# One chain of 128 features in place of two interleaved halves of 64, in the step of an LSTM

## The reference

```python
# x [32, 512, 512], cond_1024 [32, 512] is h0, Wx and Wh [512, 2048], b [2048]
xW = jnp.einsum('ntd,dg->ntg', x, Wx) + b
c0 = jnp.zeros_like(h0)
def step(carry, xw_t):
    prev_h, prev_c = carry
    a = xw_t + prev_h @ Wh
    i = jax.nn.sigmoid(a[:, :Hd])
    f = jax.nn.sigmoid(a[:, Hd:2 * Hd])
    o = jax.nn.sigmoid(a[:, 2 * Hd:3 * Hd])
    g = jnp.tanh(a[:, 3 * Hd:])
    next_c = f * prev_c + i * g
    next_h = o * jnp.tanh(next_c)
    return ((next_h, next_c), next_h)
(_, _), hs = jax.lax.scan(step, (h0, c0), jnp.swapaxes(xW, 0, 1))
return x + jnp.swapaxes(hs, 0, 1)
```

## Time and profile before

| | |
|---|---|
| time, median of 3 runs | 2726.16 us (2726.15 to 2726.85) |
| the profiled execution's own time | 2726.29 us |
| its span, first to last instruction | 2724.5 us |
| mean granted TensorE clock | 0.989 of full speed |
| TensorE matmuls, busy | 2671.2 us (98%), 49152 |
| VectorE, busy | 1929.8 us (71%), 8121 instructions |
| ScalarE, busy | 1245.7 us (46%), 3722 instructions |
| GpSimd, busy | 45.9 us (2%) |
| chain of work that ended last | TensorE 97% |
| HBM traffic | 40 GB/s over the span |

### The profile page before, as it was taken

The page is one execution under the profiler, slowest core; times in us unless marked ns, Lnnn a source line. Parts: engine busy times, 40 slices in busy tenths (PEclk is TensorE's granted clock), DMA queues, the critical chain, the costliest instruction groups (busy, mean ns, idle before and its releaser), DMA issues.

```text
span 2724.5 us, 121148 instructions
## 1 busy us (share of the span) xinstructions
PE 2671.2 (98%) x49152; PEld 1387.0 (51%) x49152; DVE 1929.8 (71%) x8121; ACT 1245.7 (46%) x3722; POOL 45.9 (2%) x134
## 2 busy tenths in 40 slices
PE   3999999999999999999999999999999999999998
PEld 0455555555555555555555555555555555555554
DVE  6777777777777777777777777777777777777776
ACT  3444444444444444444444444444444444444444
POOL 0000000000000000000000000000000000000000
PEclk6999999999999999999999999999999999999999
DMA  6111111111111111111111111111111111111111
GB/s 144 37 43 35 38 38 40 35 39 42 35 38 38 40 35 39 42 35 38 38 39 35 39 42 35 39 38 39 35 39 42 35 39 39 38 35 39 42 36 26
DMA packets 223520, 109.94 MB, mean 40 GB/s; under 512 B 25216, under 2 KB 222464, under 8 KB 222464
## 3 DMA queue, kind: packets, MB, share of 16 engines
q1 hardware_dynamic: 223488, 109.48, 15.7%
HBM read 75.83 MB, written 33.55 MB: 40 GB/s over the span
## 4 chain that ended last, share of the span: by engine, by line
PE 97%; issue 1%; DVE 1%; DMA 1%; SPq 0%; ACT 0%; POOL 0%; DVEq 0%; POOLq 0%
PE Z L244 97%; DMA wx_raw<-in_Wx 1%; DVE wh_lo L435 0%; SPq L213 0%; SPq L200 0%; DVE wmax L417 0%; SPq L208 0%; DVE h_hi L475 0%; ACT tanh_c L356 0%; POOL wmax_all L537 0%; DVE xmax L396 0%; DVE x_lo L381 0%; DVE zs L407 0%; DVE c L490 0%; DVE scales L410 0%
## 5 line engine op out<-in xcount | busy, mean ns | idle before, releaser
L350 ACT ACTIVATE act<-Z,scales 128x192 f32<-128x192 f32 x1022 | 430.9, 422 | 1159.5 <-PE Z L244 1159.5
L244 PE MATMUL Z<-wx_hi,x_hi 128*32 128x512 f16 x8176 | 807.7, 379 | 9.3 <-DVE x_lo L381 9.3
L244 PE MATMUL Z<-wh_hi,hT_hi 128*32 128x512 f16 x8176 | 808.1, 379 | 8.0 <-DVE hT_hi L480 8.0
L244 PE MATMUL Z<-wh_lo,hT_hi 128*32 128x512 f16 x8176 | 808.1, 379 | 0.0
L244 PE MATMUL Z<-wx_hi,x_lo 128*32 128x512 f16 x8176 | 807.6, 379 | 0.0
L244 PE MATMUL Z<-wx_lo,x_hi 128*32 128x512 f16 x8176 | 807.6, 379 | 0.0
L244 PE MATMUL Z<-wh_hi,hT_lo 128*32 128x512 f16 x8176 | 533.1, 379 | 0.0
L486 DVE TENSOR_TENSOR fc<-act,c 128x64 f32<-128x64 f32 x512 | 115.3, 225 | 570.2 <-ACT act L350 570.2
L356 ACT ACTIVATE tanh_c<-c 128x64 f32<-128x64 f32 x1024 | 262.3, 256 | 269.7 <-DVE c L497 249.2
L475 DVE SCALAR_TENSOR_TENSOR h_hi<-act,scales,tanh_c 128x64 f16<-128x64 f32 x1024 | 291.3, 285 | 113.1 <-ACT tanh_c L356 86.3
L327 ACT ACTIVATE Z<-bias_bc,scales 128x512 f32<-128x512 f32 x511 | 344.6, 674 | 0.0
(11 more groups left out here) (50 smaller groups left out, 1286.1 us busy)
## 6 DMA issues: line engine op xcount, KB each, us to landing
x_in<-in_x SPq DMA_DIRECT2D x512, 64.0 KB, 2.0
x_res<-in_x SPq DMA_DIRECT2D x512, 64.0 KB, 2.1
out_y<-y SPq DMA_DIRECT2D x512, 64.0 KB, 1.7
wx_raw<-in_Wx SPq DMA_DIRECT2D x16, 256.0 KB, 8.8
wh_raw<-in_Wh SPq DMA_DIRECT2D x16, 256.0 KB, 19.0
bias_bc<-in_bias SPq DMA_DIRECT2D x4, 64.0 KB, 2.0
h_in<-in_h SPq DMA_DIRECT2D x4, 16.0 KB, 13.8
```

The lines of the kernel that those rows point to most:

```text
L244: return nc.tensor.matmul(bank[L * j:L * j + B, :], lhsT, rhs, start=False, stop=last, skip_group_check=True)
L350: nc.scalar.activation(half_gates(act, a)[:, 0:3], half_gates(Z[s], a)[:, 0:3], ACT.Sigmoid, scale=scale).then_inc(sig_done, 1)
```

## The change

The chain runs once, on all 128 features. ScalarE does sigmoid on i and f together (256 columns), then tanh on g, then sigmoid on o with a semaphore of its own (`sig_o_done`), then one tanh of c. VectorE does fc, ig, c, h_hi and the transpose to hT_hi once each. TensorE waits once for hT_hi, ahead of chunk 0. The bias waits for `sig_o_done` of the bank's step before. The helpers for halves go. h32, h_lo, hT_lo, y and all work on x stay.

```diff
@@ recurrent_part (TensorE)
-                for part, ht in enumerate((hT_hi, hT_lo)):
+                for ht, ht_done, ws in ((hT_hi, hT_hi_done, (wh_hi, wh_lo)), (hT_lo, hT_lo_done, (wh_hi,))):
+                    pe.wait_ge(ht_done, t)
                     for ch in range(NCH):
-                        if part == 0 and ch % 2 == 0:
-                            pe.wait_ge(hT_hi_done, 2 * t - 1 + ch // 2)
-                        if part == 1 and ch == 0:
-                            pe.wait_ge(hT_lo_done, t)
-                        for w in ((wh_hi, wh_lo) if part == 0 else (wh_hi,)):
+                        for w in ws:
                             for j in range(NJ):
-                                mm = add(Z[s], j, ht[:, ch, :], w[:, ch, j * ZW:(j + 1) * ZW], part == 1 and ch == NCH - 1)
+                                mm = add(Z[s], j, ht[:, ch, :], w[:, ch, j * ZW:(j + 1) * ZW], ht is hT_lo and ch == NCH - 1)
@@ place_bias (ScalarE)
-                    sc.wait_ge(tanh_g_done, 2 * (t - TB) + 2)
+                    sc.wait_ge(sig_o_done, t - TB + 1)
@@ block (ScalarE)
-                    for a in range(2):
-                        nc.scalar.activation(half_gates(act, a)[:, 0:3], half_gates(Z[s], a)[:, 0:3],
-                                             ACT.Sigmoid, scale=scale).then_inc(sig_done, 1)
-                        nc.scalar.activation(half_gates(act, a)[:, 3], half_gates(Z[s], a)[:, 3],
-                                             ACT.Tanh, scale=scale).then_inc(tanh_g_done, 1)
-                    for a in range(2):
-                        sc.wait_ge(c_done, 2 * t + 1 + a)
-                        nc.scalar.activation(half(tanh_c, a), half(c, a), ACT.Tanh).then_inc(tanh_c_done, 1)
+                    nc.scalar.activation(act[:, 0:2 * C], Z[s][:, 0:2 * C], ACT.Sigmoid, scale=scale).then_inc(sig_done, 1)
+                    nc.scalar.activation(act[:, 3 * C:], Z[s][:, 3 * C:], ACT.Tanh, scale=scale).then_inc(tanh_g_done, 1)
+                    nc.scalar.activation(act[:, 2 * C:3 * C], Z[s][:, 2 * C:3 * C], ACT.Sigmoid,
+                                         scale=scale).then_inc(sig_o_done, 1)
+                    sc.wait_ge(c_done, t + 1)
+                    nc.scalar.activation(tanh_c[:, :], c[:, :], ACT.Tanh).then_inc(tanh_c_done, 1)
@@ step (VectorE); high_part_of_h, turn_high_part, half and half_gates are removed
-                v.wait_ge(sig_done, 2 * t + 1)
-                nc.vector.tensor_tensor(half(fc, 0), half_gates(act, 0)[:, 1], half(c, 0), ALU.mult)
-                ...
-                turn_high_part(t, 1)
+                v.wait_ge(sig_done, t + 1)
+                nc.vector.tensor_tensor(fc[:, :], act[:, C:2 * C], c[:, :], ALU.mult)
+                v.wait_ge(tanh_g_done, t + 1)
+                nc.vector.tensor_tensor(ig[:, :], act[:, 0:C], act[:, 3 * C:], ALU.mult).then_inc(ig_done, 1)
+                v.wait_ge(ig_done, t + 1)
+                nc.vector.tensor_tensor(c[:, :], fc[:, :], ig[:, :], ALU.add).then_inc(c_done, 1)
+                v.wait_ge(sig_o_done, t + 1)
+                v.wait_ge(tanh_c_done, t + 1)
+                nc.vector.scalar_tensor_tensor(h_hi[:, :], act[:, 2 * C:3 * C], h_scale(q), tanh_c[:, :],
+                                               ALU.mult, ALU.mult).then_inc(h_hi_done, 1)
+                v.wait_ge(h_hi_done, t + 1)
+                nc.vector.transpose(hT_hi[:, :, :], h_hi[:, :].rearrange("p (ch l) -> p ch l", ch=NCH)).then_inc(hT_hi_done, 1)
```

## The result

The changed kernel takes 2843.7 us (median, 2843.05 to 2844.78), the kernel before 2726.4 (four runs of each). The ratio is 1.043, 95% interval 1.0412 to 1.0449: 4.3% slower, 117.3 us. The profiled execution took 2843.51 us for a span of 2841.7.

A forecast was written before the change was run, and what follows sets the result against it. TensorE's own matmul stream was taken to bound the kernel. 510 steps x 0.195 us of TensorE waiting = 99.5 us, added to 2726.3, gave 2826 us (+3.7%), range 2765 to 2858.

The forecast's parts named there:

- the stall: TensorE's wait before the first hT_hi matmul in each step: 0.215 us, less 0.02 at the restart, so 0.195.
- The margin: How much later the first half of hT_hi may come before TensorE waits: 2.36 - 2.18 = 0.18 us a step.
- TensorE's wake-up: From the end of the transpose to hT_hi until the first matmul on it: 0.14 us.
- Rival A: Wide operations cheaper (ig and c at 0.25), TensorE's wake-up 0.10: 2780 us, or 2765 with smaller ScalarE slopes; chance 0.27.
- The chain's growth: From the first sigmoid to hT_hi ready: 2.435 in place of 2.04, so 0.39 us later.
- The row of h32: Profile row of the 128-wide h32 multiply on VectorE, 0.25 us, used as the lower bound for ig and c.
- restart: After its wait on hT_hi, TensorE's second matmul group follows sooner, winning back 0.02 us a step at full clock.
- the ends of the run: First recurrent matmul about 0.3 us later, low part after the last z_done turned 0.34 us earlier: they cancel.
- B: Wide operations cost more: ig at 0.29, no 0.02 gained at the restart; 0.245 us a step, 2851 us; chance 0.11 above 2849.
- C: Not slower: the wide chain grows by less than 0.18 us and fits under the input part, 2726 us; chance 0.05.
- The clock (D): Small TensorE pauses bring its clock down for a third of the time: over 3500 us; chance 0.02.
- E: First hT_hi matmul need not wait for the whole transpose, so the second half's margin absorbs it; chance within that of C.

The follow-up runs named there:

- the two delays of 0.2 and 0.8 us: Kernel before with unread VectorE work ahead of the first half's h_hi: one 512-column operation, 2829.5 us; two such operations, 3137.5 us.
- half tail: Changed kernel with tanh of c, h_hi and the hT_hi transpose in two halves, no wait for the sigmoid of o ahead of h_hi: 2726.6 us.
- the run with one wait: Changed kernel without VectorE's wait for the sigmoid of o ahead of h_hi, keeping the wait for tanh of c: 2807.2 us.

## Why the prediction was right, and where two of its steps were not

**The bound and the direction.** The question put was the right one: does the chain grow by more than its cover? It does, TensorE waits once a step ahead of the first hT_hi matmul, and each delay returns in full: 510 times 0.23 us. Forecast 2826, measured 2843.7, inside the range; the term that was wrong by 17.9 us is the stall, 0.23 where I had 0.195.

**The margin: wrong.** I took TensorE's wake-up (from the transpose's end to the first matmul on it), 0.14 us, from the only wait in the trace, that of the earlier trace rows, at half the granted clock and behind 8 us of idling. In the steady stretch it is 0.05 (the changed kernel, and the two delays of 0.2 and 0.8 us). So the margin was 2.36 - 2.04 - 0.05 = 0.27. The half tail and the delays show it. Rival A named 0.10 for this term, in the right direction and still too much.

**The chain's growth: wrong too, the other way.** 0.49 us and not 0.39. Of the missing 0.095, some 0.03 are ig: I gave it 0.26 because it starts just as fc ends; it took 0.292, the upper end of my range. c took its 0.292 as said. The row of h32 (0.25) is no price for a tensor_tensor of 128 columns that waits for its input. The Trainium skill's rule of "VectorE: DVE Perf Modes", section on the TRN2 errata, which I had weighed against that row, gives 291 ns, and fc, ig and c agree (292 to 293), while h32 and y, issued while a transpose still runs, stay at 250 in the changed kernel too. A running neighbour alone is not enough for that: ig starts 0.03 before fc's record ends (1504.34 against 1504.37) and takes 292. The other 0.065 to 0.07 are the wait written second, a term that the prediction did not have at all: it listed what the wait for the sigmoid of o waits for and called it free, and not what having it costs. The runs with the wait dropped and swapped measure it at 36 us.

**Then a small one.** I gave TensorE 0.02 us back at its restart, as the earlier trace rows suggested. At full clock the group after the first follows at 0.23 (1506.15 to 1506.38), not sooner than 0.216; that makes 0.03 with the sign turned. The three errors: 0.095 - 0.09 + 0.03 = 0.035 us a step, 18 us. That the prediction was so near is luck: two wrong terms of 0.09 cancelled.

**What went as said.** The sizes of the wide sigmoid (474 ns for 475), tanh of c (312 for 309), h_hi (352) and the transpose (311); the low part of h comes earlier and is waited for by nobody; the bias and VectorE's work for x stay free, though the bias comes 0.46 us earlier in the step (1.63 after the sigmoid's start, 2.09 before) and not 0.2 later as I wrote, because the second tanh of c ahead of it is gone; the ends of the run cancel; nothing happened to the clock.

**What I asked the profile to show, wrongly.** The idle time before the hT_hi matmuls was to be 100 to 120 us and is 31.9, since the records overlap. VectorE's and ScalarE's busy time fell to 1663 and 1064 us, not to 1500 and 1005: I added up durations, and the narrow operations overlapped each other in the records, so less busy time went than their sum. Added up as durations, VectorE's records do shrink by 429 us and ScalarE's by 242, about as worked out.

**The rivals.** B (ig at 0.29, no gain at the restart) had these two sizes about right, with 2851; it had neither the wait written second nor the short wake-up. C, that one wide chain would still fit, fails by the same chain of numbers: it would need a growth under 0.27, and the operations alone cost 0.42 (hT_hi ready at 2.46 in the run with one wait, 2.04 before). The clock (D) did not fall in any run, not with 0.8 us of stall in each 6 us; what the Trainium skill, "TensorE: Matmul & The Clock Gate", section on the second HAM failure mode, tells of small pauses is not borne out here at this length. The first transpose cut off again (0.069 us) and the half tail show that E was rightly left aside.

**Is anything faster?** No run beats the kernel before. Of the change one can keep the wide sigmoids, fc, ig and c, with halves from tanh of c on and a single wait ahead of each h_hi: the same time with fewer instructions.

## What to carry to other kernels

Cutting a dependent chain in halves pays by when the first piece arrives, not by work: fewer, wider operations saved 0.5 us of VectorE's busy time a step and cost 0.23 us of time. Before merging operations on such a chain, work out the cover from starts in the timeline, and price a wake-up from a row at the same clock and after the same kind of pause, or give both ends. Where a VectorE instruction has two waits, write the one that ends last first, or drop the one that the other covers.

## What the runs showed of the hardware that I had not expected

- Of two waits ahead of a VectorE instruction, the order counts: with the late one second, the instruction starts 0.10 us after its release (0.20 once in eight steps, in one place), with it first 0.03. Seen at 64 and 128 columns. The wait written second is an entry of its own in VectorE's queue, which the profile shows between the two.
- TensorE's wake-up behind a VectorE transpose was 0.05 to 0.06 us at full clock, for stalls of 0.2 to 0.8 us, and 0.15 after 8 us at half clock. Which of the two, the pause or the clock, makes the difference was not tried apart.
- A tensor_tensor of 128 fp32 columns is 292 ns when it waits for its input, and 250 (h32, y) when it is issued while a transpose still runs: the same shape, 42 ns apart. No run tried apart whether the neighbour or the wait makes the difference.
